# Two more groups of transposes given from TensorE to VectorE, and the mix moved to an earlier place in the tile

## The chip, the cores and the metric

One NeuronCore of a Trainium2 chip runs the whole program. The metric is the device time of the kernel in microseconds (us); the time before is a median of three runs. Engines are named as in the profile: PE is TensorE, PEld its weight loads, DVE VectorE, ACT ScalarE, POOL GpSimd, and SP the engine whose queue issues nearly all DMAs.

## The reference, cut to what matters

`x` is (128 items, 32 channels, 512). Four steps are each added to it:

```
K  = 2 * Re(sum_n Ct exp(dtA * t))             # a long convolution per channel (through FFTs), skip D, length mask
x  = x + (causal_conv(x, K) + x * D) * mask
x  = x + einsum('bct,bcd->bdt', x, W1[cond])   # a 32x32 matrix picked per item
x  = x + einsum('bct,bcd->bdt', x, W2[cond])
gate = x Wg^T + 0.5 * (x Ag^T) Bg^T            # Ag, Bg: LoRA matrices of rank 16, picked per item
up   = x Wu^T + 0.5 * (x Au^T) Bu^T
act  = silu(gate) * up                         # 1376 wide
x  = x + act Wd^T + 0.5 * (act Ad^T) Bd^T
```

## The kernel before, in words

Every product is made in three passes of fp32r matmuls (high x high, low x high, high x low), so each operand exists as a rounded "high" part, which ACT writes, and a "low" remainder, which DVE or POOL subtracts.

The first 121 us hold the convolution. After it, `tile_pe` runs 32 tiles (t = 0 to 31) of 4 items, that is 128 rows of 512. p = t mod 2 picks halves of double buffers. Tiles 0 and 1 and tiles 30 and 31 are written out, and those between run in a hardware loop over blocks of two tiles. A tile consists of these pieces on PE:

- `mix(t + 1)`, three matmuls: both channel mixes of the **next** tile in one, x1 times a block-diagonal 128x128 matrix `wbd`, into the PSUM bank `misc`. It waits for `wbd`, which four small DMAs fill (one per item, `load_wbd`), and for the high and low part of x1. ACT copies the result to `x3n` (`x3_copy`), DVE turns it with 16 transposes of 32x128 into `x3r` (`x3_turn`; a 128x512 tile is a 4x4 grid of such strips), and ACT and DVE write the high and low parts that the next tile multiplies (`x3_high`, `x3_low`).
- `chunk(p, q, u)`, twelve matmuls: gate (u = 0) or up (u = 1) of column group q. The hidden width is cut into groups 0, 1 and 2 of 352, 512 and 512 columns (`PAIRS`, `FW`). Each group has a pair of PSUM banks in `gub`, and groups 1 and 2 alternate banks with the neighbouring tiles. The first chunk is 480 wide, as it also makes the LoRA A products.
- `lora_b(t, p, q)`, four matmuls, completes gate and up of group q. Behind it ACT makes the silu and DVE the product (`act_mul`) into the single buffer `act_t`.
- `a_turn(t, q)`, three or four PE transposes, turns `act_t` into the PSUM bank `atp`. ACT and DVE make the high and low parts `ats` (`a_high`, `a_low`).
- `down(t, p, q)`, 18 or 24 matmuls of 288 columns, adds group q to the output accumulators. `lora_b_down` adds the LoRA part of the output, and `out_sum` on DVE adds x3 and gives `outb`, which SP stores.

The order is written out by hand in one function for each engine: `tile_pe`, `tile_act`, `tile_dve`, `tile_lows` (POOL) and `tile_io` (SP). Each engine runs its list strictly in order, and semaphores join them. On SP the list of a tile is: the two loads of the next x1 (`load_x`), the B matrices of group 2 (`load_b`), the A matrices (`load_ag`, `load_ad`), `load_wbd`, B of group 0 for the next tile, the store of the previous output (which waits for `out_sum`), B of group 1 for the next tile, and the output's B matrix (`load_bd`). Ahead of every block of two tiles `block_io` reads the indices of its items into registers (`entries`, four table reads with their bounds checks, L211).

```
            def block_io(i, first=False, last=False):
                here = entries(SP, i, 0, NA, 0, BB)
                there = None if last else entries(SP, i + 1, 0, NA, 0, GB)
                mixes = entries(SP, i, 1, NCOND, GB, BB)
                after = None if last else entries(SP, i + 1, 1, NCOND, 0, GB)
                ...
                tile_io(i * 2, 0, here[0:GB], here[GB:], mixes, first=first)
                tile_io(i * 2 + 1, 1, here[GB:], there, after, last=last)
```

So `wbd` for an odd tile is loaded in the SP list of the even tile before it, behind the reading of the indices, and `wbd` for an even tile in the list of the odd tile, with no such reading ahead.

## Time and profile before

| | before |
|---|---|
| median of three runs | 1070.89 us (1070.21 to 1073.7) |
| the profiled execution: its own time | 1069.72 us |
| its span, first to last instruction | 1067.9 us |
| mean granted TensorE clock | 0.997 |
| PE busy | 1037.9 us (97%), 5922 matmuls |
| DVE busy | 490.4 us (46%), 1095 instructions |
| ACT busy | 402.1 us (38%) |
| POOL busy | 484.8 us (45%) |
| DMA | 135.50 MB, mean 127 GB/s |

Busy time is a union, so overlapping instructions count once. A matmul's own duration is longer than the distance to the next one, because matmuls are pipelined: what a matmul costs is read from start to start. DMA issuing isn't counted as busy, so how full SP is can only be seen on its timeline. A row of the timeline joins like instructions (x4) and gives the first one's start and the time from there to the end of the last.

### The profile page before, as it was taken

The numbers are of one execution on the slowest core, as the hardware profiler recorded it, in microseconds if no ns is written. First come the engines' busy times: TensorE is split into PE (matmuls) and PEld (weight loads), VectorE is DVE, ScalarE is ACT, GpSimd is POOL, SyncE is SP. The second block draws the span as 40 slices with busy tenths as digits, with TensorE's granted clock in tenths as the row PEclk, the third lists the DMA queues.
The fourth block names the chain that finished last, engine by engine and source line by source line (L and its number), as shares of the span: only waits on it lengthen the run. The fifth ranks groups of instructions, "written<-read, shape, count | busy, mean of one in ns | idle before, by whom it ended". The sixth has DMA issues, their size and how long they took to land.

```text
span 1067.9 us, 19023 instructions
## 1 busy us (share of the span) xinstructions
PE 1037.9 (97%) x5922; PEld 906.3 (85%) x5922; DVE 490.4 (46%) x1095; ACT 402.1 (38%) x627; POOL 484.8 (45%) x301
## 2 busy tenths in 40 slices
PE   3999899999999999999999999999999999999998
PEld 3665688888898888888888988888888888888887
DVE  8333344545444445445454445454454444454442
ACT  7002234434433433344343334334443433443341
POOL 0605354545445444545454454445454544544441
PEclk9999899999999999999999999999999999999999
DMA  9799342424333343424243333434242433334320
GB/s 340 249 404 337 116 110 89 134 69 138 98 109 101 99 123 101 120 84 136 71 138 97 108 99 101 125 99 122 80 137 73 137 96 107 102 98 128 104 75 20
DMA packets 100980, 135.50 MB, mean 127 GB/s; under 512 B 26395, under 2 KB 59420, under 8 KB 100956
## 3 DMA queue, kind: packets, MB, share of 16 engines
q1 hardware_dynamic: 100380, 135.12, 41.3%
q8 instruction: 12, 0.20, 0.1%
q10 hardware_dynamic: 576, 0.08, 0.1%
q14 instruction: 12, 0.10, 0.0%
HBM read 118.11 MB, written 16.99 MB: 127 GB/s over the span
## 4 chain that ended last, share of the span: by engine, by line
PE 94%; DVE 3%; DMA 3%; issue 0%; ACT 0%; DVEq 0%; ACTq 0%
PE ps L984 47%; PE ps L1016 27%; PE ps L994 8%; PE ps L962 5%; PE ps L1005 4%; DMA x1p<-yo 2%; PE ps L1039 1%; PE ps L1038 1%; PE ps L975 1%; PE ps L972 1%; PE ps L973 1%; DVE x3r L815 0%; DMA tr<-kpad 0%; DVE xs L704 0%; PE ps L936 0%; PE ps L1027 0%
## 5 line engine op out<-in xcount | busy, mean ns | idle before, releaser
L984 PE MATMUL ps<-wg_hi,x_hi 128*128 128x512 f32 (+2 forms) x768 | 299.2, 390 | 4.6 <-DVE x_lo L805 4.6
L984 PE MATMUL ps<-wg_lo,x_hi 128*128 128x512 f32 (+2 forms) x768 | 291.7, 380 | 0.0
L984 PE MATMUL ps<-wg_hi,x_lo 128*128 128x512 f32 (+2 forms) x768 | 290.7, 379 | 0.0
L471 POOL TENSOR_TENSOR bst<-braw,bst 128x1024 fp32r<-128x1024 f32 (+1 forms) x96 | 212.7, 2215 | 90.7 <-ACT bst L572 90.7
L815 DVE STREAM_TRANSPOSE x3r<-x3n 32x128 f32<-32x128 f32 x512 | 155.0, 303 | 92.3 <-ACT x3n L545 85.8
L588 ACT ACTIVATE at_hi<-ps 128x512 fp32r<-128x512 f32 (+1 forms) x95 | 53.4, 562 | 315.1 <-PE ps L1005 315.1
L984 PEld LDWEIGHTS ps<-wg_hi,x_hi 128*128 128x128 f32 x768 | 145.1, 189 | 25.9 <-issue 4.7
L984 PEld LDWEIGHTS ps<-wg_hi,x_lo 128*128 128x128 f32 x768 | 145.1, 189 | 25.2
L984 PEld LDWEIGHTS ps<-wg_lo,x_hi 128*128 128x128 f32 x768 | 145.3, 189 | 20.4
L1016 PE MATMUL ps<-wd_hi,at_hi 128*128 128x288 f32 x696 | 151.9, 300 | 0.0
L1016 PE MATMUL ps<-wd_lo,at_hi 128*128 128x288 f32 x696 | 149.0, 296 | 0.0
L1016 PE MATMUL ps<-wd_hi,at_lo 128*128 128x288 f32 x696 | 148.5, 295 | 0.0
L1016 PEld LDWEIGHTS ps<-wd_hi,at_hi 128*128 128x128 f32 x696 | 113.4, 188 | 14.9 <-DVE at_lo L848 12.3
L461 POOL TENSOR_TENSOR wg_lo<-agraw,wg_hi 128x256 fp32r<-128x256 f32 x64 | 58.2, 930 | 147.5 <-ACT wg_hi L558 147.5
L466 POOL TENSOR_TENSOR wd_lo<-adraw,wd_hi 128x704 fp32r<-128x704 f32 x32 | 66.8, 2088 | 124.7 <-ACT wd_hi L565 124.7
L1016 PEld LDWEIGHTS ps<-wd_hi,at_lo 128*128 128x128 f32 x696 | 112.1, 189 | 0.0
L1016 PEld LDWEIGHTS ps<-wd_lo,at_hi 128*128 128x128 f32 x696 | 111.6, 188 | 0.0
L583 ACT ACTIVATE act_t<-ps 128x512 f32<-128x512 f32 (+1 forms) x96 | 52.6, 548 | 151.6 <-PE ps L994 151.6
L572 ACT ACTIVATE bst<-braw,odd 128x1024 fp32r<-128x1024 f32 (+1 forms) x96 | 103.1, 1073 | 0.0
L848 DVE TENSOR_TENSOR at_lo<-ps,at_hi 128x512 fp32r<-128x512 f32 (+1 forms) x95 | 61.5, 647 | 79.4 <-ACT at_hi L588 78.5
L452 POOL TENSOR_TENSOR x_raw<-x_raw,xb 128x512 f32<-128x512 f32 x31 | 40.0, 1292 | 127.5 <-DMA xb<-in_x 127.5
L842 DVE TENSOR_TENSOR act_t<-act_t,ps 128x512 f32<-128x512 f32 (+1 forms) x96 | 60.3, 628 | 46.4 <-ACT act_t L583 46.4
(147 smaller groups left out, 1184.6 us busy)
## 6 DMA issues: line engine op xcount, KB each, us to landing
braw<-in_tb SPq DMA_DIRECT2D x256, 128.0 KB, 2.7
braw<-in_tb SPq DMA_DIRECT2D x128, 96.0 KB, 2.4
adraw<-in_tad SPq DMA_DIRECT2D x128, 88.0 KB, 1.9
tr<-kpad SPq DMA_DIRECT2D x16, 512.0 KB, 6.9
x1p<-yo SPq DMA_DIRECT2D x16, 512.0 KB, 5.7
xb<-in_x SPq DMA_DIRECT2D x32, 256.0 KB, 2.8
agraw<-in_ta SPq DMA_DIRECT2D x128, 64.0 KB, 2.0
bdraw<-in_tbd SPq DMA_DIRECT2D x128, 64.0 KB, 2.2
```

What stands on the lines that cost most here:

```text
L461: last = sub(ag_view(wg_lo, u), ag_from(u), ag_view(wg_hi, u).bitcast(F32), ALU.subtract)
L466: sub(ad_view(wd_lo, p), ad_from(), ad_view(wd_hi, p).bitcast(F32), ALU.subtract).then_inc(s["adlo"], 1)
L471: sub(v, b_from(p, q), v.bitcast(F32), ALU.subtract).then_inc(s["blo"], 1)
L572: copy(b_view(p, q), b_from(p, q), ACT.Copy, scale=odd[:, 0:1]).then_inc(s["bhi"], 1)
L588: copy((ats[0] if to is None else to)[:, 0:n * P], atp[:, 0:n * P], ACT.Copy).then_inc(s["ahi"], 1)
L815: last = V.transpose(turned, part)
L842: tt(act_t[:, 0:w], act_t[:, 0:w], gub[2 * ((p + q) % 2) + 1][:, 0:w], ALU.mult).then_inc(s["mul"], 1)
L848: tt(lo[:, 0:n * P], atp[:, 0:n * P], hi[:, 0:n * P].bitcast(F32), ALU.subtract).then_inc(s["alo"], 1)
L962: last = mm(yp[h % 4][:, c * P:T], u_pair(q)[:, h % 2, c * P:(c + 1) * P], tr[:, q % NTP, h % 2, 0:T - c * P], start=(c == 0), stop=(c == ...
L984: last = mm(bank[:, 0:n], x3s[a][:, k, :], wgs[b][:, k, o:o + n], start=(k == 0 and a + b == 0), stop=False, skip_group_check=True)
L994: last = mm(gub[2 * ((p + q) % 2) + u][:, 0:w], ts2[a][:, u, :], bst[:, (p + q) % 2, u * n:u * n + w], start=False, stop=(a == 1), skip_gr ...
L1016: last = mm(acc[h], ats[a][0:m, (j - j0) * P:(j - j0 + 1) * P], wds[b][0:m, j, o:o + DH], start=(q == 0 and j == j0 and a + b == 0), stop= ...
```

## The change

On PE, `a_turn(t - 1, 2)` and `a_turn(t, 1)` are gone, except for the last tile's group 2. `mix(t + 1)` moves from ahead of `down(t, p, 0)` to directly behind `lora_b(t, p, 0)`, and `down(t - 1, 2)` moves behind it. On DVE a function `turn` makes the two turned groups with 16 transposes each, from `act_t` into the PSUM bank `atp`. The transposes of x3 now go into the PSUM bank `misc` (where mix put x3, and from where ACT has meanwhile copied it to a new buffer `x3m`), in three parts between other steps. `x3_high` and `x3_low` read `misc`, and a second ACT copy, `x3_keep`, fills `x3n`. ACT, DVE and POOL get new orders. SP's list is as it was.

```diff
@@ POOL: tile_lows
                     x_sum(t + 1)
+                    x1_low(t + 1)
                 b_low(t, p, 1)
                 if not last:
                     ag_low(t + 1)
-                    x1_low(t + 1)
@@ ACT
-            def x3_copy(t, p):
+            def x3_copy(t):
                 act.wait_ge(s["x3mm"], t + 1)
-                copy(x3n[:, p, :], misc, ACT.Copy).then_inc(s["x3n"], 1)
+                copy(x3m[:], misc, ACT.Copy).then_inc(s["x3n"], 1)
+
+            def x3_keep(t, p, free=None):
+                act.wait_ge(s["x3n"], t + 1)
+                if free is not None:
+                    act.wait_ge(s["evac"], free)
+                copy(x3n[:, p, :], x3m[:], ACT.Copy).then_inc(s["x3k"], 1)
...
             def a_high(t, q, to=None):
-                act.wait_ge(s["att"], t * 3 + q + 1)
+                if q == 0:
+                    act.wait_ge(s["att"], t + 1)
+                elif to is not None:
+                    act.wait_ge(s["att"], NT + 1)
+                else:
+                    act.wait_ge(s["dn"], t * 2 + q)
+                    act.wait_ge(s["atv"], t * 2 + q)
@@ ACT: tile_act
                 t_high(t)
+                if not last:
+                    x1_high(t + 1)
                 b_high(t, p, 1, None if first else t * 3)
                 silu(t, p, 0)
+                if not last:
+                    x3_copy(t + 1)
+                    ag_high(t + 1)
+                a_high(t, 0)
                 if not first:
                     td_high(t - 1)
-                a_high(t, 0)
-                if not last:
-                    ag_high(t + 1)
-                    x1_high(t + 1)
                 b_high(t, p, 2, t * 3 + 1)
                 silu(t, p, 1)
                 bd_high(t, first)
                 if not last:
-                    x3_copy(t + 1, 1 - p)
-                a_high(t, 1)
-                if not last:
+                    x3_keep(t + 1, 1 - p, None if first else t)
                     ad_high(t + 1, 1 - p, None if first else t)
                     b_high(t + 1, 1 - p, 0, t * 3 + 2)
+                a_high(t, 1)
+                if not last:
                     x3_high(t + 1, t * 3 + 3)
@@ DVE
+            def turn(to, of, blocks):
+
+                for i, j in blocks:
+                    rows, cols = slice(i * C, (i + 1) * C), slice(j * C, (j + 1) * C)
+                    last = V.transpose(to[cols].rearrange("f (k n) -> f k n", n=P)[:, :, rows],
+                                       of[rows].rearrange("n (k f) -> n k f", f=P)[:, :, cols])
+                return last
...
+            def a_turn(t, q):
+                dve.wait_ge(s["mul"], t * 3 + q + 1)
+                turn(atp, act_t[:], GRID).then_inc(s["atv"], 1)
@@ DVE: tile_dve
                     act_mul(t - 1, 1 - p, 2)
+                    a_turn(t - 1, 2)
                 t_mask(t, p)
                 t_turn(t)
                 if not first:
                     a_low(t - 1, 2)
                 t_low(t)
+                act_mul(t, p, 0)
+                if not last:
+                    x3_turn(t + 1, GRID[0:8])
                 if not first:
                     td_mask(t - 1, 1 - p)
                     td_turn(t - 1)
-                act_mul(t, p, 0)
+                if not last:
+                    x3_turn(t + 1, GRID[8:12])
                 if not first:
                     td_low(t - 1)
+                if not last:
+                    x3_turn(t + 1, GRID[12:16], True)
                 a_low(t, 0)
                 if not first:
                     out_sum(t - 1, 1 - p, None if second else (t - 1) * 16)
                 act_mul(t, p, 1)
-                if not last:
-                    x3_turn(t + 1, 1 - p)
+                a_turn(t, 1)
                 a_low(t, 1)
@@ PE: tile_pe
                 chunk(p, 0, 0).then_inc(s["la"], 1)
-                if not first:
-                    a_turn(t - 1, 2)
                 chunk(p, 0, 1)
                 if not first:
-                    down(t - 1, 1 - p, 2)
+                    pe.wait_ge(s["mul"], t * 3)
+                chunk(p, 1, 0)
                 pe.wait_ge(s["tlo2"], t + 1)
                 lora_b(t, p, 0)
-                chunk(p, 1, 0)
+                if not last:
+                    mix(t + 1, 1 - p)
+                if not first:
+                    down(t - 1, 1 - p, 2)
                 a_turn(t, 0)
...
-                if not last:
-                    mix(t + 1, 1 - p)
                 pe.wait_ge(s["adlo"], t + 1)
                 down(t, p, 0)
-                a_turn(t, 1)
                 chunk(p, 2, 1)
```

PE, where the mix stands in a tile. Before, between the last chunk of group 2's gate (L984) and `down` of group 0 (L1016):

```order
L984 MATMUL ps<-wg_hi,x_hi 128x512
L984 MATMUL ps<-wg_lo,x_hi 128x512
L984 MATMUL ps<-wg_hi,x_lo 128x512
L972 MATMUL ps<-x_hi,wbd 128x512 [waits s_wbd,s_x1hi,s_evac]
L973 MATMUL ps<-x_hi,wbd 128x512
L975 MATMUL ps<-x_lo,wbd 128x512 [waits s_x1lo]
L1016 MATMUL ps<-wd_hi,at_hi 128x288 [waits s_alo,s_adlo]
```

Now, behind the four matmuls of `lora_b` of group 0 (L1026) and ahead of `down` of the previous tile's group 2 (L1048):

```order
L1026 MATMUL ps<-bst,t_hi 128x352 [waits s_blo,s_tlo2]
L1026 MATMUL ps<-bst,t_lo 128x352
L1026 MATMUL ps<-bst,t_hi 128x352
L1026 MATMUL ps<-bst,t_lo 128x352
L1004 MATMUL ps<-x_hi,wbd 128x512 [waits s_wbd,s_x1hi]
L1005 MATMUL ps<-x_hi,wbd 128x512
L1007 MATMUL ps<-x_lo,wbd 128x512 [waits s_x1lo]
L1048 MATMUL ps<-wd_hi,at_hi 128x288 [waits s_alo]
```

The mix is now passed by three chunks, a `down` and the LoRA part of the output that used to stand ahead of it, and it keeps its wait on `wbd`.

SP, between the odd tile's last DMA (`bdraw`) and the even tile's first (`x_raw`), before and now alike:

```order
L332 DMA bdraw<-in_tbd 32x1x512
L426 UNCONDITIONAL_BRANCH
L426 ISA
L211 TENSOR_LOAD ixs
L211 ISA x17
L211 TENSOR_LOAD ixs
L211 ISA x9
L211 TENSOR_LOAD ixs
L211 ISA x9
L211 TENSOR_LOAD ixs
L211 ISA x8
L300 ISA [waits s_x3mm]
```

Nothing moved here: the reading of the indices stands where it did.

DVE, from the product of group 1 (L867) on, now:

```order
L867 TENSOR_TENSOR act_t<-act_t,ps 128x512 [waits s_silu]
L827 STREAM_TRANSPOSE ps<-act_t 32x4x32 [waits s_mul]
L827 STREAM_TRANSPOSE ps<-act_t 32x4x32 x15
L873 TENSOR_TENSOR at_lo<-ps,at_hi 128x512 [waits s_ahi]
L820 TENSOR_TENSOR x_lo<-ps,x_hi 128x512 [waits s_x3hi]
```

Before, the sixteen transposes at this place were those of x3 (`x3r<-x3n`); now they are those of the activations, into PSUM, and x3's stand further up.

## Rows read from the trace of the kernel before

**Rows 1.** PE's timeline at a tile's start: start us, us, engine, line, operation.
```profile
531.61 0.38 PE L984 MATMUL ps<-wg_hi,x_hi 128*128 128x480 f32 x1
...
536.55 0.42 PE L1016 MATMUL ps<-wd_hi,at_hi 128*128 128x288 f32 x2
...
539.75 0.32 PE L994 MATMUL ps<-bst,t_hi 128*128 128x352 f32 x1
...
540.39 0.39 PE L984 MATMUL ps<-wg_hi,x_hi 128*128 128x512 f32 x1
...
543.14 0.49 PE L1005 MATMUL ps<-cs,act_t 128*128 128x128 f32 x3
...
550.41 0.39 PE L972 MATMUL ps<-x_hi,wbd 128*128 128x512 f32 x1
```
**Rows 2.** The page, part 5, and single lines: durations ns min/median/max.
```profile
L1005 PE MATMUL ps<-cs,act_t 128*128 128x128 f32 (+1 forms) x352 | 54.1, 272 | 0.0
L815 DVE STREAM_TRANSPOSE x3r<-x3n x512: 298/303/308, 114.5 to 1027.3; 32x128 f32<-32x128 f32 x171
L785 DVE TENSOR_SCALAR ps<-cs x1: 272/272/272, 29.9 to 29.9; 128x128 f32<-128x128 f32 x1
```
**Rows 3.** PE's timeline around one `a_turn` of four transposes.
```profile
504.81 0.60 PE L1005 MATMUL ps<-cs,act_t 128*128 128x128 f32 x4
...
505.41 0.32 PE L984 MATMUL ps<-wg_lo,x_hi 128*128 128x352 f32 x1
505.57 0.32 PE L984 MATMUL ps<-wg_hi,x_lo 128*128 128x352 f32 x1
```
**Rows 4.** PE's timeline ahead of `down` of group 1, at a tile's end.
```profile
498.57 0.39 PE L994 MATMUL ps<-bst,t_lo 128*128 128x512 f32 x1
498.92 0.53 PE L1016 MATMUL ps<-wd_hi,at_hi 128*128 128x288 f32 x2
```
**Rows 5.** DVE's timeline: the sixteen transposes of x3.
```profile
522.49 5.05 DVE L815 STREAM_TRANSPOSE x3r<-x3n 32x128 f32<-32x128 f32 x16 [2.71 <-ACT x3n L545]
```
**Rows 6.** SP's timeline from an odd tile's store to the even tile's `wbd`.
```profile
518.56 0.37 SPq L338 DMA_DIRECT2D out_x<-outb  x1
521.71 2.79 SPq L324 DMA_DIRECT2D braw<-in_tb  x4
524.72 2.82 SPq L332 DMA_DIRECT2D bdraw<-in_tbd  x4
535.20 0.34 SPq L300 DMA_DIRECT2D x_raw<-x1p  x1
...
543.83 2.84 SPq L294 DMA_DIRECT2D wbd<-tm_d  x4
```
**Rows 7.** SP's timeline from the even tile's B loads to the odd tile's `wbd`.
```profile
551.12 2.79 SPq L324 DMA_DIRECT2D braw<-in_tb  x4
...
557.65 0.38 SPq L301 DMA_DIRECT2D xb<-in_x  x1
560.30 2.83 SPq L324 DMA_DIRECT2D braw<-in_tb  x4
...
567.68 2.87 SPq L294 DMA_DIRECT2D wbd<-tm_d  x4
```
**Rows 8.** Tile `wbd`: the time from a DMA's issue to its landing.
```profile
DMA to landing us min/median/max: 1.9/2.0/9.0
```
**Rows 9.** Two stretches ahead of and in tile 0: window, busy, PEclk, DMA.
```profile
116.60:121.10 4.50, 0.00 (x0) 0.00 (x0) 3.47 (x11) 1.45 (x2) 0.03 (x1) 0.85 0.01 2
121.10:126.60 5.50, 5.46 (x14) 4.65 (x15) 0.28 (x1) 0.00 (x0) 1.79 (x1) 0.50 0.67 208
```
**Rows 10.** First matmuls of tiles 0 and 1 on PE's timeline.
```profile
121.14 0.74 PE L984 MATMUL ps<-wg_hi,x_hi 128*128 128x480 f32 x1 [4.57 <-DVE x_lo L805]
...
149.20 0.38 PE L984 MATMUL ps<-wg_hi,x_hi 128*128 128x480 f32 x1
```
**Rows 11.** SP's timeline: the `wbd` load in tile 0.
```profile
132.46 2.88 SPq L294 DMA_DIRECT2D wbd<-tm_d  x4
```

More of the change, by code:

```diff
@@ L169, in cond_resid_kernel @@
         x3s = [sb("x3_hi", [P, KT, TN], F32R), sb("x3_lo", [P, KT, TN], F32R)]
-        x3r = sb("x3r", [P, T])
+        x3m = sb("x3m", [P, T])
         act_t = sb("act_t", [P, T])
@@ L185, in cond_resid_kernel @@
             ag aghi aglo ad adhi adlo b0 b1 bhi blo bd bdhi bdlo
-            bfree la tm tmt thi2 tlo2 gu silu mul att ahi alo td tdm tdt tdhi tdlo accd evac ost""".split() + [
+            bfree la tm tmt thi2 tlo2 x3k gu silu mul att atv dn ahi alo td tdm tdt tdhi tdlo accd evac ost""".split() + [
             f"wl{n}" for n in range(NW)] + [f"u{q}" for q in range(C // 2)]
@@ L550, in x3_high @@
                     act.wait_ge(s["gu"], free)
-                copy(x3s[0][:].rearrange("p k n -> p (k n)"), x3r[:], ACT.Copy).then_inc(s["x3hi"], 1)
+                copy(x3s[0][:].rearrange("p k n -> p (k n)"), misc, ACT.Copy).then_inc(s["x3hi"], 1)
             def ag_high(t, first=False):
@@ L603, in _ @@
             act.wait_ge(s["yst1"], 16 * C // 4)
-            x3_copy(0, 0)
+            x3_copy(0)
             x3_high(0)
+            x3_keep(0, 0)
             act.wait_ge(s["msk"], 1)
@@ L625, in tile_act @@
                 if not last:
-                    x3_copy(t + 1, 1 - p)
+                    x3_keep(t + 1, 1 - p, None if first else t)
+                    ad_high(t + 1, 1 - p, None if first else t)
+                    b_high(t + 1, 1 - p, 0, t * 3 + 2)
                 a_high(t, 1)
                 if not last:
-                    ad_high(t + 1, 1 - p, None if first else t)
-                    b_high(t + 1, 1 - p, 0, t * 3 + 2)
                     x3_high(t + 1, t * 3 + 3)
@@ L804, in x3_low, with x3_turn @@
                 dve.wait_ge(s["x3hi"], t + 1)
-                tt(x3s[1][:].rearrange("p k n -> p (k n)"), x3r[:], x3s[0][:].rearrange("p k n -> p (k n)").bitcast(F32),
+                tt(x3s[1][:].rearrange("p k n -> p (k n)"), misc, x3s[0][:].rearrange("p k n -> p (k n)").bitcast(F32),
                    ALU.subtract).then_inc(s["x3lo"], 1)
-            def x3_turn(t, p):
-                dve.wait_ge(s["x3n"], t + 1)
-                for i in range(GB):
-                    for j in range(GB):
-                        part = x3n[i * C:(i + 1) * C, p, :].rearrange("n (k f) -> n k f", f=P)[:, :, j * C:(j + 1) * C]
-                        turned = x3r[j * C:(j + 1) * C, :].rearrange("f (k n) -> f k n", n=P)[:, :, i * C:(i + 1) * C]
-                        last = V.transpose(turned, part)
-                last.then_inc(s["x3t"], 1)
+            def turn(to, of, blocks):
[4 more added lines that the diff above has]
+                return last
+            GRID = [(i, j) for i in range(GB) for j in range(GB)]
+            def x3_turn(t, part, done=False):
+                dve.wait_ge(s["x3n"], t + 1)
+                last = turn(misc, x3m[:], part)
+                if done:
+                    last.then_inc(s["x3t"], 1)
+            def a_turn(t, q):
+                dve.wait_ge(s["mul"], t * 3 + q + 1)
+                turn(atp, act_t[:], GRID).then_inc(s["atv"], 1)
             def t_mask(t, p):
@@ L863, in out_sum @@
                 dve.wait_ge(s["accd"], t + 1)
+                dve.wait_ge(s["x3k"], t + 1)
                 if stored is not None:
@@ L875, in _ @@
             tt(x1_lo[:], xa[:], x1_hi[:].bitcast(F32), ALU.subtract).then_inc(s["x1lo"], 1)
-            x3_turn(0, 0)
+            x3_turn(0, GRID, True)
             x3_low(0)
@@ L1017, in down @@
                                       start=(q == 0 and j == j0 and a + b == 0), stop=False, skip_group_check=True)
-                if q == 2:
-                    last.then_inc(s["td"], 1)
+                if blocks is None:
+                    last.then_inc(s["td" if q == 2 else "dn"], 1)
             def down_half(h, blocks):
```

## The prediction

> **What bounds the kernel now.** The profile's first part has PE busy for 97% of the span, so I read PE's timeline over one tile and count each piece from start to start. Tile 14 begins at 531.61 and the mix at 550.41, 18.80 us into it [rows 1]. From the first matmul of tile 1 at 149.20 [rows 10] to that of tile 14, thirteen tiles later, a tile takes 29.42 us. PE leaves only one small hole in it: the last `lora_b` matmul starts at 498.57 and `down` of group 1 at 498.92 [rows 4], 0.35 us where 0.23 is usual (a chunk of twelve, 540.39 to 543.14 [rows 1], is 2.75). `down` waits 0.12 us there for `a_low`. So whatever is taken off PE is a gain, as long as nothing PE waits for becomes late. The second reading is therefore of what PE waits for, above all where the mix goes: its matrix `wbd` comes from SP, whose load of issuing no busy share shows. Its timeline [rows 6, 7] shows it going through its list with few pauses.
>
> **The turns that leave PE.** Four transposes start at 504.81, the second matmul behind them at 505.41, the third at 505.57 [rows 3]. That is 0.60 us for the turn and one matmul worth 0.16, so 0.44 us for four transposes. 252 of 352 go: 31 turns of group 2 and 32 of group 1, 63 x 0.44 = 27.7 us.
>
> The page gives the same instruction 272 ns, and 54.1 us busy for all 352 [rows 2]; durations overlap, and it is the starts that count. The Trainium skill (TensorE: Matmul & The Clock Gate, "Part 4: PE-mode transpose") has a transpose at about 275 ns in one kernel, most of it access latency; the trace agrees on the duration. If each cost that in sequence, the 252 would be worth 68.5 us and not 27.7; this is a rival below.
>
> **What DVE takes over.** A turn is 16 transposes, 5.05 us [rows 5], 32 of them more in a tile, about 10 us on an engine that is busy 46% of the time. The nearest rows for the new form are 303 ns for 32x128 within SBUF and 272 ns for a 128x128 write into PSUM [rows 2]; I take 5.05 us and bound it by 4.4 (0.272 each) and by 6.6, an estimate of 0.1 us more each for PSUM. Group 1, by the new order: the mix at +7.9 (below) takes 0.7, `down` 3.2, a turn 0.3, a chunk 2.75, the LoRA pieces 0.5 and 0.9, so its `lora_b` ends near +16.4; two chunks, a `down` of 18 and a `lora_b` (8.8 in all) put its `down` at +25.2. In between, silu and product end near +17.9, the turn at +23.0, the high and low part at +24.4 (estimates from ACT and DVE steps of 0.5 to 0.7 us). So this just fits, with 0.8 us to spare, and the hole of 0.12 us closes: 31 x 0.12 = 3.7 us. Group 2's turn ends at about +4 in the next tile, and its `down` now comes at 8.6: covered. If the cover is gone (transposes 0.05 us slower) each further 0.1 us on a transpose costs about 1.6 us in each tile.
>
> The Trainium skill (VectorE: DVE Perf Modes, "Rules for kernel authors") says to transpose 128x128 on TensorE if a PSUM destination is fine, as here. Taken at its word, with each turn at 5.05 us in place of 0.44, the 63 turns would cost 290 us more; in this kernel DVE's time is off PE's path, and I give that end no chance.
>
> A tile with no other wait would be 29.42 - 0.88 - 0.12 = 28.4 us.
>
> **The mix meets its matrix.** In the new order the mix stands behind chunks 0/gate, 0/up, 1/gate and one `lora_b`. Today the end of that `lora_b` is 8.78 us into the tile (540.39), with a turn (0.44) and a `down` (539.75 - 536.55 = 3.20) ahead that leave and a chunk (2.75) that comes [rows 1]: 8.78 - 0.44 - 3.20 + 2.75 = +7.9. It was at +18.8.
>
> When is `wbd` there? SP's list has not changed, and its anchor is the store, which waits for `out_sum`. For the even tile 14 the chain is [rows 6]: store of the odd tile 13 at 518.56 (+16.4), B loads 521.71, `bdraw` 524.72, then nothing from 527.54 to 535.20 while the indices are read, x, B, A, and `wbd` at 543.83. From B loads to `wbd` 22.12 us. The four `wbd` DMAs take 2.84 to issue; the last starts some 0.56 before that ends and lands 2.0 later [rows 8]: 4.28. So it lands at 548.1, +16.5, ahead of a mix at +18.8, by 2.3 us.
>
> New: `out_sum` stands on DVE behind all sixteen transposes of x3, which begin after the mix and its copy at about +9.4; 5.05 us of transposes and about 2.5 of short steps put the store at +17.0 of the odd tile (an estimate; if all were as today, 16.4). The B loads follow 0.8 later rather than 3.15 (today they wait for POOL's `b_low`, which comes earlier now): +17.8. `wbd` has landed at 17.8 + 22.1 + 4.3 = 44.2, less a tile of 28.4: +15.8 of the even tile. The mix is due at +7.9, so **PE waits 7.9 us in each even tile**, with all of its list behind the mix.
>
> For an odd tile the indices aren't read on the way: B loads to `wbd` is 567.68 - 551.12 = 16.56, of which 560.30 - 557.65 = 2.65 has 1.9 us of waiting that falls away [rows 7]: 14.66. 17.8 + 14.7 + 4.3 - 28.4 = +8.4: a wait of 0.5 us.
>
> In tile 0 `wbd` is issued at 132.46 [rows 11], landing at 136.8; the mix would be at 121.14 + 7.9 + 2.8 (slow clock, next paragraph) = 131.8: 5.0 us of waiting.
>
> **The clock.** PE stood idle for 4.57 us ahead of tile 0 [rows 10]. In that stretch the granted clock had a mean of 0.85, and for the 5.50 us from the tile's start it was 0.50 [rows 9], the level of 1.2 GHz. That is 2.75 us of work lost. A wait of 7.9 us is longer than this one, so I count 2.8 us more for each such wait. Bounds: 0 (no fall), and 3.4 (0.85 of 4.5 us hides another 1.35 us at half clock; all 6.85 us behind the wait would lose 3.4).
>
> **The sum.**
> - turns off PE: -27.7; hole closed: -3.7
> - 15 even tiles (2 to 30) x 7.9 = +118.5
> - the clock after them: 15 x 2.8 = +42.0
> - 14 odd tiles (3 to 29) x 0.5 = +7.0
> - tile 0: 5.0 + 2.8 = +7.8
> - the later places of the other steps (POOL's `x1_low`, ACT's `ag_high`, the extra copy `x3_keep` of 0.6 us): 0. POOL and ACT are idle over half of the time, and PE needs their results later than `wbd`. If the table were early, the first to be late would be `x1_low`, about 0.5 us ahead of its use.
> - `x3_low` reads PSUM and is off the path: 0
>
> Total +143.9 on the profiled execution's 1069.72: 1213.6. The median of the runs is 1.2 us above that execution; I predict 1214.
>
> **Rivals.**
> - *The table is in time* (faster). For it: everything else in the schedule fits, and `wbd` is 8 KB for each DMA. Then only the first two terms are left, 1069.7 - 31.4 = 1038. It decides when `wbd` lands before +7.9, so SP would have to run 8 us ahead of the chain of rows 6, past a store that waits for `out_sum`. Against it: nothing in the change moves an SP row. 0.05.
> - *The waits come, the clock doesn't fall.* Without 42.0 + 2.8: 1169. Against it: the one idle stretch of this size in the trace did have the fall [rows 9]. 0.12.
> - *DVE becomes the bound as well*: transposes into PSUM 0.1 us slower, so that 16 of them add 1.6 us ahead of `down` of group 1 and of the store, in 31 tiles: 1214 + 50 = 1264. From 0.05 us on it decides. 0.08.
> - *A PE transpose was worth its full duration*, 68.5 us: 1214 - 41 = 1173. Against it: rows 3 show the starts. 0.02.
>
> **How the numbers follow.** My forecast has 0.72; 0.01 is left for an end within 0.3% of the time before (about what a measurement of this kernel can tell from no change). The range takes in the case without the fall of the clock at its lower end, and above the upper bound of the clock (15 x 0.6 = 9) and half of the slower transposes: 1164 to 1246. Faster 0.05, same 0.01, slower 0.94.
>
> **What would show it.** Right: PE waits on the mix's line for the DMA of `wbd`, some 8 us in every second tile and under 1 us in the others; tiles alternate between about 39 and 29 us; PEclk falls to 0.5 behind each long wait; transposes of about 0.3 us; 100 PE transposes left. Wrong: no idle time of PE ahead of the mix, or a wait for x1 or DVE in its place.

## The result, and the profile after

The changed kernel takes 1210.32 us (median of four runs, 1205.85 to 1213.67), the kernel before 1070.55 on the same chip (1069.31 to 1073.7). The ratio is 1.1298, with a 95% interval of 1.1252 to 1.1344. The change makes the kernel 13% slower. The profiled execution has a span of 1211.8 us against 1067.9, and a mean granted clock of 0.932 against 0.997.

The page after, its busy times, two rows of its slices and the chain that ended last:

```profile
PE 1052.7 (87%) x5670; PEld 921.1 (76%) x5670; DVE 770.5 (64%) x2103; ACT 421.3 (35%) x659; POOL 484.8 (40%) x301
PE   3999797979889797979889797979889797979998
PEclk9999898989989898989989898989989898989989
SPq 42%; PE 19%; DVE 16%; issue 14%; DMA 7%; ACT 1%; DVEq 0%; ACTq 0%
```

PE did lose the transposes (5922 matmuls were 5670 afterwards), and DVE took them (1095 instructions, now 2103). But PE's share of the span fell from 97% to 87%, with 7s all along its row, and the granted clock dips to 8 tenths in the same rhythm. The chain is now that of SP's queue. An engine that issues DMAs and shows no busy time at all sets the end.

The longest of PE's waits: who was waited for, us in total, times, longest.

```profile
PE ps L1004 <- DMA wbd<-tm_d: 127.2, 30, 8.3
```

All of the loss hangs on one line, the first matmul of the mix (L1004), and one tile, `wbd`. PE's timeline of an even tile (12, from 526.18) and the odd one behind it (13, from 565.49); the number in brackets is the idle time ahead:

```profile
526.18 0.38 PE L1016 MATMUL ps<-wg_hi,x_hi 128*128 128x480 f32 x1
...
533.91 0.32 PE L1026 MATMUL ps<-bst,t_lo 128*128 128x352 f32 x1
542.28 0.80 PE L1004 MATMUL ps<-x_hi,wbd 128*128 128x512 f32 x1 [8.05 <-DMA wbd<-tm_d]
...
565.49 0.38 PE L1016 MATMUL ps<-wg_hi,x_hi 128*128 128x480 f32 x1
...
573.22 0.32 PE L1026 MATMUL ps<-bst,t_lo 128*128 128x352 f32 x1
573.97 0.50 PE L1004 MATMUL ps<-x_hi,wbd 128*128 128x512 f32 x1 [0.42 <-DMA wbd<-tm_d]
```

The even tile waits 8.05 us and is 39.31 us long. The odd one waits 0.42 and is 29.0 long (tile 14 begins at 594.49). The even tiles 2 to 28 wait 7.6 to 8.4 us; tile 30 waits only 4.95 and tile 0 4.41, as will be seen below. Behind the long wait the clock is at its lower level (stretch: its length, busy time of PE, PEld, DVE, ACT and POOL, PEclk, DMA share, GB/s):

```profile
534.23:538.00 3.77, 0.00 (x1) 0.00 (x0) 0.52 (x1) 1.73 (x3) 3.35 (x2) 1.00 0.60 155
538.00:542.28 4.28, 0.00 (x0) 0.00 (x0) 0.00 (x0) 0.00 (x0) 0.22 (x1) 0.50 0.19 47
542.28:548.10 5.82, 5.82 (x22) 5.53 (x23) 2.57 (x8) 1.73 (x3) 1.66 (x2) 0.50 0.25 68
```

The grant falls to 0.50 (1.2 GHz of 2.4) while PE still waits, and PE then works for 5.82 us at half speed: up to 2.9 us lost for each such wait. SP's timeline, from the even tile's store to its `wbd` and on to the next one, shows why the table comes when it does; it answers to [rows 6, 7]:

```profile
554.27 0.37 SPq L338 DMA_DIRECT2D out_x<-outb  x1
554.97 2.78 SPq L324 DMA_DIRECT2D braw<-in_tb  x4
...
569.61 2.86 SPq L294 DMA_DIRECT2D wbd<-tm_d  x4
...
583.37 0.37 SPq L338 DMA_DIRECT2D out_x<-outb  x1
584.07 2.79 SPq L324 DMA_DIRECT2D braw<-in_tb  x4
587.08 2.82 SPq L332 DMA_DIRECT2D bdraw<-in_tbd  x4
597.57 0.34 SPq L300 DMA_DIRECT2D x_raw<-x1p  x1
...
606.19 2.84 SPq L294 DMA_DIRECT2D wbd<-tm_d  x4
```

From B loads to `wbd` it is 606.19 - 584.07 = 22.12 us with the reading of the indices (the hole of 7.7 us ahead of 597.57), as before, and 569.61 - 554.97 = 14.64 us without it. The change moved the mix forward by 11 us, and nothing on SP moved with it.

On DVE the transposes into PSUM take 323 ns each, sixteen of them 5.37 us, where they took 303 ns and 5.05 us into SBUF [rows 5]. The page's groups, and the turn of group 1 in tile 12 with what follows it:

```profile
L827 DVE STREAM_TRANSPOSE ps<-act_t 32x128 f32<-32x128 f32 x1008 | 325.4, 323 | 14.9
L827 DVE STREAM_TRANSPOSE ps<-x3m 32x128 f32<-32x128 f32 x512 | 165.2, 323 | 147.1 <-ACT x3m L545 139.6
```

```profile
555.03 5.37 DVE L827 STREAM_TRANSPOSE ps<-act_t 32x128 f32<-32x128 f32 x16
561.13 0.69 DVE L873 TENSOR_TENSOR at_lo<-ps,at_hi 128x512 fp32r<-128x512 f32 x1 [0.73 <-ACT at_hi L600]
```

### The profile page after: what moved, and what is told of

Its sections match the earlier page's. It is cut to its first block, busy times and chain, and to the rows that moved or that the text cites. A ratio compares the mean times of both kernels' runs of the same rounds, so it can differ in the third digit from the quotient of the medians.

```text
span 1211.8 us, 19793 instructions
## 1 busy us (share of the span) xinstructions
PE 1052.7 (87%) x5670; PEld 921.1 (76%) x5670; DVE 770.5 (64%) x2103; ACT 421.3 (35%) x659; POOL 484.8 (40%) x301
## 4 chain that ended last, share of the span: by engine, by line
SPq 42%; PE 19%; DVE 16%; issue 14%; DMA 7%; ACT 1%; DVEq 0%; ACTq 0%
SPq L324 13%; DVE ps L827 9%; PE ps L1048 8%; SPq L211 6%; SPq L332 6%; SPq L294 5%; DMA wbd<-tm_d 5%; PE ps L994 4%; SPq L307 4%; SPq L314 4%; PE ps L1016 3%; PE ps L1004 2%; DMA x1p<-yo 2%; SPq L338 1%; SPq L300 1%
## 5 line engine op out<-in xcount | busy, mean ns | idle before, releaser
L827 DVE STREAM_TRANSPOSE ps<-act_t 32x128 f32<-32x128 f32 x1008 | 325.4, 323 | 14.9
L1016 PE MATMUL ps<-wg_hi,x_hi 128*128 128x512 f32 (+2 forms) x768 | 294.4, 383 | 4.9 <-DVE x_lo L820 4.9
L1016 PE MATMUL ps<-wg_lo,x_hi 128*128 128x512 f32 (+2 forms) x768 | 291.4, 379 | 0.0
L1016 PE MATMUL ps<-wg_hi,x_lo 128*128 128x512 f32 (+2 forms) x768 | 291.1, 379 | 0.0
L827 DVE STREAM_TRANSPOSE ps<-x3m 32x128 f32<-32x128 f32 x512 | 165.2, 323 | 147.1 <-ACT x3m L545 139.6
L1016 PEld LDWEIGHTS ps<-wg_hi,x_hi 128*128 128x128 f32 x768 | 145.3, 189 | 26.5 <-issue 5.0
L1016 PEld LDWEIGHTS ps<-wg_hi,x_lo 128*128 128x128 f32 x768 | 145.0, 189 | 25.3
L1016 PEld LDWEIGHTS ps<-wg_lo,x_hi 128*128 128x128 f32 x768 | 145.3, 189 | 21.5
L1048 PE MATMUL ps<-wd_hi,at_hi 128*128 128x288 f32 x696 | 161.4, 316 | 0.2 <-DVE at_lo L873 0.2
L1048 PE MATMUL ps<-wd_lo,at_hi 128*128 128x288 f32 x696 | 160.4, 314 | 0.0
L1048 PE MATMUL ps<-wd_hi,at_lo 128*128 128x288 f32 x696 | 159.1, 312 | 0.0
L1048 PEld LDWEIGHTS ps<-wd_hi,at_hi 128*128 128x128 f32 x696 | 130.8, 211 | 10.0 <-DVE at_lo L873 0.7
L1004 PE MATMUL ps<-x_hi,wbd 128*128 128x512 f32 x32 | 20.5, 641 | 127.7 <-DMA wbd<-tm_d 127.2
L867 DVE TENSOR_TENSOR act_t<-act_t,ps 128x512 f32<-128x512 f32 (+1 forms) x96 | 60.4, 629 | 104.2 <-ACT act_t L589 102.8
L1048 PEld LDWEIGHTS ps<-wd_hi,at_lo 128*128 128x128 f32 x696 | 122.9, 206 | 0.0
L1048 PEld LDWEIGHTS ps<-wd_lo,at_hi 128*128 128x128 f32 x696 | 122.9, 207 | 0.0
L1004 PEld LDWEIGHTS ps<-x_hi,wbd 128*128 128x128 f32 x32 | 7.5, 234 | 136.9 <-DMA wbd<-tm_d 126.1
```

The costliest lines, as they stand in the source:

```text
L827: last = V.transpose(to[cols].rearrange("f (k n) -> f k n", n=P)[:, :, rows], of[rows].rearrange("n (k f) -> n k f", f=P)[:, :, cols])
L867: tt(act_t[:, 0:w], act_t[:, 0:w], gub[2 * ((p + q) % 2) + 1][:, 0:w], ALU.mult).then_inc(s["mul"], 1)
L1016: last = mm(bank[:, 0:n], x3s[a][:, k, :], wgs[b][:, k, o:o + n], start=(k == 0 and a + b == 0), stop=False, skip_group_check=True)
L1048: last = mm(acc[h], ats[a][0:m, (j - j0) * P:(j - j0 + 1) * P], wds[b][0:m, j, o:o + DH], start=(q == 0 and j == j0 and a + b == 0), stop= ...
```

## The experiments

All theories start from this one: PE waits for `wbd`, because the mix moved ahead of SP's list; the clock falls behind the wait; the rest of the change is a gain of about 1 us in each tile. The rival for the whole is that the early mix or DVE's new work costs by itself. The runs first test the clock, then move the table in three steps, then take the change apart. Each kernel is the changed one with the edit shown, unless another is named.

### Dummy matmuls in the wait

```diff
                 lora_b(t, p, 0)
                 if not last:
+                    if p == 0:
+                        keep_warm(misc, 40 if first else 56)
                     mix(t + 1, 1 - p)
```

The 56 extra matmuls write `misc`, which the mix then overwrites.

> The changed kernel with 56 dummy matmuls of 256 columns (40 in tile 0) ahead of the mix in every even tile, into the bank that the mix overwrites: PE works through most of the wait for wbd, so only the clock is changed. If the fall of the clock is a price of its own behind the idle time (my theory): PEclk stays at 1.00 behind the mix, even tiles shorten from 39.2 us to about 36.4, the odd ones stay at 29.0, and the time is 1210 - 16 x 2.8 = about 1166 us. If the clock costs nothing, since the matmuls behind the mix would be held by something else anyway: 1210 us as before. If the clock falls for another reason than the idle time, PEclk still shows 0.50 there and the time stays near 1210.

Measured: 1182.45 us (1180.26 to 1184.31), ratio 1.1041 (1.1017 to 1.1065), clock 0.992. The gain is 27.9 us between the medians (31.3 between the two profiled executions). PE's wait for `wbd` is 27.8 us in all, since the rest of it is now filled. Twelve of the fifteen even tiles (6 to 28) went from about 39.2 to 36.6 us, 2.6 each or 32 us; they still have 1.2 to 1.4 us of idle time behind the dummies, and the clock stays at 1.00 behind it. Tile 30 gained 1.1: its wait was only 4.95 us, and the dummies take 6.9. Tiles 2 and 4 gained nothing; there the dummies ended 1.8 and 2.0 us ahead of the table, and the clock fell all the same (tile 2):

```profile
200.73 1.00 PE L978 MATMUL ps<-wg_hi 128*128 128x256 f32 x7
203.54 0.71 PE L1004 MATMUL ps<-x_hi,wbd 128*128 128x512 f32 x1 [1.81 <-DMA wbd<-tm_d]
```

```profile
203.60:207.00 3.40, 3.40 (x12) 3.12 (x13) 1.19 (x4) 1.72 (x3) 0.06 (x1) 0.51 0.42 116
```

The run was expected at 1166 us and missed that by 16: the 44 us of gain took all fifteen even tiles and tile 0 to gain 2.8 each. So the fall of the clock is real and is worth 2.6 us in a tile. The work that PE does in the wait changes nothing else: the table comes as late as ever, 16.2 us into tile 12.

### The table ahead of x in SP's list

```diff
             def tile_io(t, p, here, there, mixes, first=False, last=False):
                 if not last:
+                    load_wbd(t if not first else None, mixes, 1 - p)
                     load_x(t + 1)
                     ...
-                    load_wbd(t if not first else None, mixes, 1 - p)
```

> The changed kernel with the wbd load moved ahead of x, B and A in SP's list of a tile, still behind the reading of the indices. If SP's order is what holds the mix: wbd lands about 8.4 us earlier, at +7.5 of the even tile, and the wait passes to x1, whose DMAs now follow wbd by 3.1 us: x_sum, x1_high and x1_low end near +13, so that PE waits about 4.6 us in an even tile, odd tiles run without a wait at 28.4. 1069.7 - 31 + 15 x 4.6 + 4 = about 1112 us, and up to 1150 if the clock still falls behind a wait of this length. If the waits come from DVE's fuller list instead (the rival), moving an SP load changes little: above 1190 us.

Measured: 1131.34 us (1130.58 to 1133.51), ratio 1.057 (1.055 to 1.059). It removes 79 us of the 140. PE's first wait has a new name:

```profile
PE ps L1004 <- ACT x_hi L541: 50.8, 16, 3.7
PE ps L1007 <- POOL x_lo L456: 4.5, 8, 0.6
```

The table is no longer late, and x1 is, since its two loads now stand behind the table's four on the same queue. SP has too little lead for either: what is put first is in time, and what is put behind it is late. The wait is 3.4 to 3.7 us in each of the even tiles 2 to 28, with the clock at 0.50 behind it (5.11 us from 506.89 on), and two short ones make up the 16; the odd tiles are 28.3 us long, those even ones 34.2 to 35.5. The time lies between the 1112 us expected without a fall of the clock and the 1150 with one.

### The table two tiles ahead

`wbd` for tile t + 2 is loaded in the list of tile t, the indices for it are read ahead with their block, and the two halves of the buffer have a semaphore each.

```diff
-                    load_wbd(t if not first else None, mixes, 1 - p)
+                    if mixes is not None:
+                        load_wbd(t + 1, mixes, p)
```

> The changed kernel with wbd loaded for the tile after next at the same place in SP's list (the buffer of that parity is free since the last mix; a semaphore for each of the two buffers). wbd is then a tile early. If the table was the only late thing apart from x1: in even tiles x1's low part ends near +9.8, 1.5 us behind its use, so even tiles take 29.9 us, odd ones 28.4, no fall of the clock, and the time is 1069.7 - 31 + 15 x 1.5 + 2 = about 1063 us. If DVE's list or ACT's (the rival) were late by itself, the tiles stay above 31 us and the time above 1120.

Measured: 1062.56 us (1062.19 to 1063.48), ratio 0.9923 (0.9906 to 0.994): 0.8% less than the kernel before. The waits for the table are gone but for one, in tile 0. x1 is late by half a microsecond in the even tiles 2 to 28, first its high part from ACT and then its low part from POOL, and these tiles take 29.5 to 29.9 us where the odd ones take 28.32:

```profile
PE ps L1010 <- POOL x_lo L459: 7.7, 14, 0.5
PE ps L1007 <- ACT x_hi L544: 5.4, 14, 0.5
PE ps L1007 <- DMA wbd<-tm_d: 5.4, 1, 5.4
```

### x two tiles ahead as well

```diff
-                if not last:
+                if not last and first:
                     load_x(t + 1)
...
                         load_wbd(t + 1, mixes, p)
+                    if mixes is not None:
+                        load_x(t + 2)
```

> As the one before, and the loads of x1 for the tile after next stand directly behind wbd as well (both x buffers are free once the mix of the next tile is done). If SP's list is the whole of the loss: every tile takes 28.4 us, PE waits nowhere in the loop, PEclk 1.00 throughout, and the time is 1069.7 - 31 = about 1039 us, under both kernels. If something else is late (the rival: the transposes into PSUM, which take 323 ns, leave a_low of group 1 no room), tiles stay above 29.4 us and the time at or above 1070.

Measured: 1045.1 us (1042.78 to 1046.99), ratio 0.9757 (0.9734 to 0.978). Every tile from 1 on is 28.32 us long. What is left is tile 0, at 35.0 us: its mix waits 6.20 us for its table, which still stands in SP's list of tile 0 itself, and the tile takes 6.9 us more than in the next kernel, where it doesn't wait. That is why 1045 was measured and not the 1039 expected.

### The first two tables before the tiles

To the kernel of the last section, `wbd` for tile 1 is loaded along with that for tile 0, under the convolution, and x of tile 1 first thing.

```diff
-            mixes = entries(SP, 0, 1, NCOND, 0, GB)
+            mixes = entries(SP, 0, 1, NCOND, 0, BB)
...
-                    load_wbd(None, mixes, 0)
+                    load_wbd(None, mixes[0:GB], 0)
+                    load_wbd(None, mixes[GB:], 1)
```

> As the version with wbd and x1 two tiles ahead, and wbd for tile 1 is loaded with tile 0's during the convolution, x1 of tile 1 ahead of the first B load. If tile 0's 35.0 us are the same wait for wbd (6.2 us) and the clock behind it: tile 0 takes about 27.6 us and the time is 1045 - 7.4 = 1038 us. If tile 0 is long for another reason (the slow clock of its start, loads of the first A and B), under 2 us are gained.

Measured: 1037.21 us (1036.53 to 1038.61), ratio 0.9688 (0.9661 to 0.9715). The prediction had a rival in which the table is in time, at 1038 us, and here that number is met within 1 us. But the rival took everything else in the schedule to fit, and that isn't so: with the table early and x where it was, the time was 1062.56. It takes x two tiles ahead as well, and both tables ahead of tile 0, to get there. The first matmuls of two tiles in succession:

```profile
518.66 0.38 PE L1018 MATMUL ps<-wg_hi,x_hi 128*128 128x480 f32 x1
...
546.98 0.38 PE L1018 MATMUL ps<-wg_hi,x_hi 128*128 128x480 f32 x1
```

28.32 us from start to start, and no waits for a DMA in the tiles.

### The turns back on PE in that kernel

```diff
                 chunk(p, 0, 0).then_inc(s["la"], 1)
+                if not first:
+                    a_turn(t - 1, 2)
                 chunk(p, 0, 1)
...
                 down(t, p, 0)
+                a_turn(t, 1)
                 chunk(p, 2, 1)
```

DVE's two turns go out, and ACT waits for PE's again.

> As the version before in this call, with the turns of groups 1 and 2 on TensorE. Without waits in the way, the price of the turns shows: 63 x 0.44 = 28 us more by start-to-start distances, so 1066 us, tiles of 29.2 us. If a transpose is worth its duration of 272 ns: 68 us more, 1106. If DVE's turns gain nothing because DVE is late with them (the rival): 1038 to 1045.

Measured: 1062.93 us (1062.49 to 1064.49), ratio 0.9925 (0.9898 to 0.9951). Tiles are 29.18 us long:

```profile
530.31 0.38 PE L1010 MATMUL ps<-wg_hi,x_hi 128*128 128x480 f32 x1
...
559.50 0.38 PE L1010 MATMUL ps<-wg_hi,x_hi 128*128 128x480 f32 x1
```

So with SP out of the way, the 63 turns are worth 1062.93 - 1037.21 = 25.7 us, or 0.41 each. The rest of the change is worth 0.24 us in each tile, 29.42 - 29.18, and 7.6 us from tile 0 to tile 31: the closed hole of 0.12 us, and 0.10 that PE took longer to get going behind it. In the kernel before, the second pair of matmuls behind the hole starts at 499.29, 0.37 us after the first at 498.92, where 0.27 is usual.

### The mix alone: turns back on PE, SP as in the change

The same edit, made to the changed kernel itself.

> The changed kernel with the turns of groups 1 and 2 back on TensorE, at their old places; the mix stays at its new place and SP's list as it is. PE then has 63 x 0.44 = 28 us more work. If SP's list sets the even tiles (my theory), most of that work fits into the time that PE waits for wbd: even tiles stay at 39.2, odd ones go from 29.0 to 29.3, and the time is 1215 us. If the turns' 28 us are simply on top (the sum taken term by term), 1238 us. If DVE's own load had caused the waits (the rival), the time falls below 1190.

Measured: 1213.74 us (1212.23 to 1214.63), ratio 1.1337 (1.1307 to 1.1367). PE does 26 us more work here than in the changed kernel, and the time is the same within the intervals: the median is 3.4 us longer, and from the first matmul of tile 0 to that of tile 31 both traces take 1052.8 us. The wait has shrunk in its place, by 16 us:

```profile
PE ps L996 <- DMA wbd<-tm_d: 111.0, 18, 7.2
```

Tiles 13 and 14 start at 562.97 and 592.15: the odd tile is 29.18 long, as in the kernel with the turns on PE and SP out of the way, and waits for nothing. The even one before it is 38.95. The pair takes 592.15 - 524.02 = 68.1 us here and 594.49 - 526.18 = 68.3 in the changed kernel. Both are one round that closes through SP: from the even tile's mix to the odd tile's `out_sum` and store, and down SP's list to the next table. The first part of it is 41.0 us here (539.61 to 580.61) and 41.1 there (542.28 to 583.37), but it takes another way. The chain that ended last, here:

```profile
PE 43%; SPq 27%; issue 11%; DVE 11%; DMA 5%; POOL 2%; ACT 1%; DVEq 0%; POOLq 0%
```

Here it goes over PE's chunks between the even tile's mix and the odd one's, since the odd tile waits for no table. In the changed kernel it was SP 42% and PE 19%: there the odd tile's mix waits for its table too, so the chain runs from the even mix over one `down` and DVE to the store at 554.27, down SP's list to the odd tile's table, over DVE again to the store at 583.37 and down the list once more. PE's chunks aren't on it at all, and taking a turn off them shortens nothing. The terms of the sum, turns and waits, are not independent. With the turns on DVE, PE only arrives at the wait earlier.

### The mix back in its place, the turns on DVE

```diff
-                if not last:
-                    mix(t + 1, 1 - p)
                 if not first:
                     down(t - 1, 1 - p, 2)
...
                     pe.wait_ge(s["wlo"], 9)
+                if not last:
+                    mix(t + 1, 1 - p)
                 pe.wait_ge(s["adlo"], t + 1)
```

ACT's copy of x3 moves behind the silu of group 1, and DVE's turn of x3 behind that of group 1 (`a_low` of group 1 between its fourth and its fifth transpose).

> The mix goes back to its place behind chunk 2/gate, all else stays as in the change (both turns on DVE, x3's turn into PSUM, SP's list). Theory: the table lands near +16 of an even tile and the mix is due near +19.2, so PE no longer waits for wbd. But DVE then has two turns behind one another late in the tile: the product of group 1 near +17.9, its turn to +23.3, x3's turn to +28.7, and ACT's and DVE's high and low part to about +30.9, where a tile without waits is 28.4 long. So PE waits some 2.5 us for x_lo at the start of every tile, no tile alternates with the next, and the time is 1038 + 31 x 2.5 = 1116 (range 1085 to 1140). With the clock at half for a stretch behind each of these waits it would be up to 1160. Rival: DVE has room for both, x_lo is in time, and the early mix was never needed: 1038 to 1050. Second rival: the table is late here too (SP's list is behind the later out_sum): tiles alternate again and the time is above 1150.

Measured: 1111.64 us (1111.3 to 1112.28), ratio 1.0386 (1.0369 to 1.0403), clock 0.997, and all tiles but the first between 30.60 and 30.78 us long. PE no longer waits for the table at all. It waits for DVE:

```profile
PE ps L1013 <- DVE x_lo L820: 52.5, 32, 4.9
PE ps L1023 <- DVE t_lo L862: 12.0, 31, 0.4
```

```profile
538.73 5.36 DVE L827 STREAM_TRANSPOSE ps<-act_t 32x128 f32<-32x128 f32 x16
544.13 1.33 DVE L827 STREAM_TRANSPOSE ps<-x3m 32x128 f32<-32x128 f32 x4
545.36 0.67 DVE L873 TENSOR_TENSOR at_lo<-ps,at_hi 128x512 fp32r<-128x512 f32 x1
546.06 4.03 DVE L827 STREAM_TRANSPOSE ps<-x3m 32x128 f32<-32x128 f32 x12
550.83 0.69 DVE L820 TENSOR_TENSOR x_lo<-ps,x_hi 128x512 fp32r<-128x512 f32 x1 [0.74 <-ACT x_hi L557]
```

DVE works from the product of group 1 to the end of the tile with hardly a gap, and x_lo is ready at 551.52, 1.55 us after PE wants it. This is what the early mix is for, in this order of DVE's list; no other was tried. The two halves of the change belong together, and the early mix needs a third one, on SP, which is missing.

### x3 turned into SBUF again

In the kernel with all tables ahead, `x3_turn` writes a buffer `x3r` in SBUF rather than `misc`.

```diff
-                last = turn(misc, x3m[:], part)
+                last = turn(x3r, x3m[:], part)
```

> As the best version, but x3 is turned into an SBUF buffer, as before the change, so that x3_low has two SBUF operands. If POOL's subtractions at that time block it again (2.13 us in place of 0.69), the product of group 2 and its turn start 1.4 us later, t_low becomes late for the first lora_b by 0.5 us and x1's low part by 0.3: tiles of 29.1 us and 1038 + 31 x 0.8 = 1062 us. If the PSUM destination doesn't matter, 1038 us, or a little less, as a transpose within SBUF takes 303 ns and not 323.

Measured: 1035.67 us (1034.28 to 1037.74), ratio 0.9667 (0.9641 to 0.9694), the same as with PSUM within the intervals. The theory missed. It held that `x_lo` from two operands in SBUF takes 2.13 us, as it did in the kernel before. It takes 0.69 here:

```profile
516.96 0.69 DVE L823 TENSOR_TENSOR x_lo<-x3r,x_hi 128x512 fp32r<-128x512 f32 x1 [1.25 <-ACT x_hi L560]
```

POOL's neighbouring rows in that kernel, from `x_raw` to its next operation:

```profile
514.55 1.30 POOL L455 TENSOR_TENSOR x_raw<-x_raw,xb 128x512 f32<-128x512 f32 x1
525.63 1.29 POOL L459 TENSOR_TENSOR x_lo<-x_raw,x_hi 128x512 fp32r<-128x512 f32 x1 [9.79 <-ACT x_hi L544]
```

POOL is idle when DVE gets there. In the kernel before it was not. There the same operation began 0.26 us after one of POOL's and ended 0.55 us after it:

```profile
528.79 1.84 POOL L471 TENSOR_TENSOR bst<-braw,bst 128x768 fp32r<-128x768 f32 x1
```

```profile
529.05 2.13 DVE L805 TENSOR_TENSOR x_lo<-x3r,x_hi 128x512 fp32r<-128x512 f32 x1 [0.79 <-ACT x_hi L551]
```

The Trainium skill has the rule (SBUF — State Buffer, "SBUF: two separate sides"): a DVE operation with two SBUF inputs and a GpSimd operation that reads SBUF share a port pair, and the later of them waits until the other is through. By that rule the trace agrees in both kernels: 2.13 us beside POOL, 0.69 without it.

### x3 into PSUM alone, in the kernel before

To see that rule at work, and the last part of the change by itself, the kernel before with x3's turn into `misc`, and the two readers of it there.

```diff
-                        turned = x3r[j * C:(j + 1) * C, :]...
+                        turned = misc[j * C:(j + 1) * C, :]...
```

> The kernel before, with one part of the change alone: x3's sixteen transposes write PSUM, and ACT's high part and DVE's low part (x_lo) read it there. Theory: x_lo took 2.13 us in the kernel before because DVE had two operands in SBUF and POOL was in the middle of an operation on SBUF (1.84 us, begun 0.26 us before); with one operand in PSUM it takes 0.69 us although POOL is still at work, and the transposes take 0.32 us each in place of 0.30. The two nearly cancel into DVE and PE waits for neither, so the time stays: 1070 +- 3. Rival: the 2.13 us have to do with something else (the output's form, or the order of DVE's list), and x_lo stays near 2.1 us. Second rival: x3 was on the path after all, and the time falls by 31 x 1.1 = 34 us, to 1036.

Measured: 1080.94 us (1079.42 to 1082.32) against 1069.57 (1067.75 to 1071.64) of the kernel before, ratio 1.0104 (1.0088 to 1.0121). The mechanism is as the theory had it: `x_lo` is at 0.69 us although POOL is at work (532.69, the same `bst`). But the time is not. It is 11 us longer, 1% and clear of the interval, which none of the three cases of the expectation has.

```profile
526.41 5.37 DVE L814 STREAM_TRANSPOSE ps<-x3n 32x128 f32<-32x128 f32 x16 [2.71 <-ACT x3n L544]
531.80 0.69 DVE L847 TENSOR_TENSOR at_lo<-ps,at_hi 128x512 fp32r<-128x512 f32 x1
532.93 0.69 DVE L804 TENSOR_TENSOR x_lo<-ps,x_hi 128x512 fp32r<-128x512 f32 x1 [0.44 <-ACT x_hi L550]
```

```profile
532.69 1.86 POOL L470 TENSOR_TENSOR bst<-braw,bst 128x768 fp32r<-128x768 f32 x1
```

```profile
532.55 0.53 PE L1015 MATMUL ps<-wd_hi,at_hi 128*128 128x288 f32 x2 [0.28 <-DVE at_lo L847]
PE ps L1015 <- DVE at_lo L847: 8.9, 31, 0.3
```

The low part of group 1 (`at_lo`) stands behind x3's sixteen transposes in DVE's list, and `down` of group 1 waits for it. That was the small hole of [rows 4]. The 0.32 us that the PSUM destination adds to sixteen transposes passes straight through it: tiles are 29.74 us long in place of 29.42, and 31 x 0.32 = 10 us. What the shorter `x_lo` gives back lies behind that point and is worth nothing: PE waits for `x_lo` in neither kernel's loop. "The two nearly cancel" was wrong because only one of them was on the path.

## Why the prediction was right

Its forecast of 1214 us has 1210.3 beside it. The mechanism is the one that was forecast, and each term is right in sign and in size to a few microseconds; that the total comes so close is in part luck, as the errors of the terms (1.4 and 3.3 us too high, 3.1 too low) nearly cancel. The terms are read in the profiled executions, 1213.67 us after and 1069.72 before. From the first matmul of tile 0 to that of tile 31 it was 1031.70 - 121.14 = 910.56 us before; it is 1176.54 - 123.76 = 1052.78 after, and 1000.10 - 122.38 = 877.72 in the kernel with the tables ahead:

```profile
1176.54 0.38 PE L1016 MATMUL ps<-wg_hi,x_hi 128*128 128x480 f32 x1
```

```profile
1000.10 0.38 PE L1018 MATMUL ps<-wg_hi,x_hi 128*128 128x480 f32 x1
```

- **Turns and hole, -31.4 forecast.** 877.72 - 910.56 = -32.8. A tile without waits was to be 28.4 us and is 28.32. The reading from start to start, 0.44 us for four transposes, is borne out by the kernel that puts them back (0.41 a turn). The rival of the full duration, 68.5 us for the 252, is off by a factor of 2.7.
- **Waits for `wbd`, 130.5 forecast** (118.5 + 7.0 + 5.0). 127.2 (116.6 + 6.3 + 4.4). The steps behind it were met nearly to the tenth. In the odd tile: B loads to `wbd` 14.64 us (14.66), landing at +8.5 (+8.4), wait 0.42 (0.5). In the even tile: 22.12 (22.12), landing at +16.1 (+15.8), wait 8.05 (7.9). The store comes at +17.9 in place of +17.0, of which the transposes into PSUM are 0.3 us; against that, the odd tile is 29.0 long and not 28.4 (the prediction gave it a wait of 0.5 and left that out here), so the two errors partly cancel. Tile 30 was counted like the others and waits 4.95: SP's list of the last block is without the indices of a next one, and from B loads to `wbd` it takes 1148.47 - 1130.01 = 18.5 us. Tile 0 waits 4.41 rather than 5.0.
- **The clock, 44.8 forecast.** Of 1052.78 - 877.72 = 175.1, what is left beside the waits is 47.9 us, but not all of it is the clock. 42.9 are in the 15 even tiles, 2.9 each, 3.8 in the odd tiles, 0.25 each, and 1.1 in tile 0. In the odd tiles the clock is at 1.00: a wait costs a little more than the idle time that the profile gives for it. In tile 13 the matmul behind it starts 0.75 us after the one ahead (573.22 to 573.97), where 0.16 for that one and 0.42 of wait make 0.58, and the next is 0.33 behind (574.30), where 0.23 is usual. The even tiles' 2.9 us are then some 2.6 of clock and 0.25 of this, and 2.6 us a tile is what came back in the run with dummies. So the clock was taken 0.2 too high in a tile and 1.7 or more in tile 0, and a term for PE getting going again was missing; the two nearly cancel.
- **DVE.** Transposes were taken at 5.05 us for sixteen, between 4.4 and 6.6. They take 5.37. The low part of group 1 was to be ready at +24.4. It is, at 561.13 + 0.69 - 526.18 = +35.6 less 8.05 of waiting and 2.9 of slow clock, +24.7, and `down` of group 1 doesn't wait for it any more (0.2 us in all). The margin forecast at 0.8 us is 0.5 in tile 12 and 0.4 in tile 13.
- **The steps costed at nothing** were nothing in this kernel: in its tiles PE waits for none of them, POOL's, ACT's or the new `x3_keep`. The prediction named `x1_low` as the next to be late once the table is early, but still in time by 0.5 us. In the kernel with the table two tiles ahead it comes 0.5 us too late, and x's high part, which hangs on the same two loads, as much. So the rival in which the table is in time would not have given 1038 by itself.

Two more things it did not have. Its sum adds the gain of the turns and the cost of the waits as if each stood for itself. The mix alone would then be 1210.3 + 27.7 = 1238; it is 1213.7. The round of two tiles closes through SP, and whatever PE does less of within it becomes waiting. The total came out right because every term was worked out for this one kernel. (From its sum to its forecast there is a slip as well: 1213.6 and 1.2 make 1214.8, and not 1214.) And it gave x3's PSUM destination no cost, "off the path"; in the kernel before it costs 0.32 us a tile, and in the changed order, where x3's transposes stand well ahead of the low part of group 1, it is hidden: with the tables ahead, x3 in PSUM or in SBUF gives the same time. With SP's list mended, sixteen DVE transposes of 5.37 us are the cheaper choice against 0.41 us of PE, since PE is the bound and DVE (74% busy) is not. The Trainium skill's advice to transpose 128x128 on TensorE where a PSUM destination will do (VectorE: DVE Perf Modes, "Rules for kernel authors") does not hold here: the measurement of 1037.21 against 1062.93 us decides.

The fastest kernel is the change with SP's list mended: table and x loaded two tiles ahead, and the first two tables ahead of the tiles. It takes 1037.21 us, or 1035.67 with x3 in SBUF, which is 3.1 to 3.3% less than the kernel before and 14% less than the changed one.

## What to carry to other kernels

- When a step moves forward in one engine's list, ask for each of its inputs who delivers it and when, counted from that deliverer's own list. The input that was 2 us early is 8 us late when its consumer moves by 11, and a queue that only issues DMAs shows no busy time to warn of it.
- A late input on a bound engine costs its wait and what comes behind it, here 8 us and 2.9, of which some 2.6 are the clock; and while it lasts, work taken off that engine gains nothing. Mend the supply first, measure savings afterwards.
- A small wait that is there already (0.12 us) marks a chain without slack. Anything longer ahead of it in another engine's list can pass straight through, as 0.32 us x 31 did.

## What the runs showed of the hardware that was not expected

- Transposes of 32x128 fp32 on DVE take 323 ns into PSUM (314 to 335) and 303 ns into SBUF (298 to 310), in every kernel here: 5.37 and 5.05 us for sixteen.
- A PE transpose of 128x128 that is 272 ns long on the page costs about 0.10 us from start to start in a run of matmuls.
- The granted clock fell behind an idle time of 1.81 and one of 2.01 us (tiles 2 and 4 of the run with dummies). It did not fall behind 1.2 to 1.4 us in the twelve even tiles after them, nor behind 1.45 to 1.55 us at the start of 31 tiles of the kernel with the late mix (mean 0.997). An idle time as short as 1.8 us was not forecast to matter. What PE did ahead of it differs too (dummies of 256 columns in the one kernel, full tiles in the other), and no run tells the length of the idle time and what stood ahead of it apart.
- A DVE operation with both operands in SBUF took 2.13 us when begun within an operation of POOL, and 0.69 with POOL idle. With one operand in PSUM it took 0.69 beside the same operation of POOL.
- A wait of PE costs about 0.25 us more than the idle time that the profile gives for it, at the full clock (the 14 odd tiles 3 to 29 of the changed kernel).
